# Second expert layer on the chosen pairs alone: rows scattered by expert through DRAM, in blocks of 128

## What is computed

```python
def _L1_ffn_ref(x, router_w, w1, w2, w3):     # 8 experts, hidden size 341
    logits = flat @ router_w.T
    probs = softmax(logits)
    topk_probs, topk_idx = top_k(probs, 2)
    topk_probs = topk_probs / (sum(topk_probs) + 1e-09)
    gates = einsum('nk,nke->ne', topk_probs, one_hot(topk_idx))
    h = silu(einsum('nc,ehc->neh', flat, w1)) * einsum('nc,ehc->neh', flat, w3)
    y = einsum('neh,ech->nec', h, w2)
    out = einsum('ne,nec->nc', gates, y)
```

## Time and profile before

| | before |
|---|---|
| median of 3 runs | 553.89 us (552.29 to 556.23) |
| span of the profiled execution | 552.8 us |
| PE busy | 487.0 us (88%), 1884 matrix instructions |
| DVE busy | 388.4 us (70%) |
| ACT busy | 268.6 us (49%) |
| POOL busy | 117.0 us (21%) |
| chain that ended last | PE 55%, DVE 24%, ACT 10%, issue 8% |

### The profile page before, as it was taken

How to read it: one execution, slowest core, us unless ns; L and a number is a source line. 1 busy time by engine, 2 the same in 40 slices (tenths; PEclk the granted TensorE clock), 3 DMA queues, 4 the chain that set the end, 5 groups by cost and what they waited for, 6 DMA issues and landing times.

```text
span 552.8 us, 6153 instructions
## 1 busy us (share of the span) xinstructions
PE 487.0 (88%) x1884; PEld 300.3 (54%) x1884; DVE 388.4 (70%) x709; ACT 268.6 (49%) x443; POOL 117.0 (21%) x171
## 2 busy tenths in 40 slices
PE   5496789868799989999799999899898998998996
PEld 3332545435356744556344444335466886776896
DVE  1997989766576832257648959767877967778674
ACT  5988787678675521032431222202225556565553
POOL 4000000000010000000000000885203554546564
PEclk9689589989799999989999999979998999999999
DMA  8880000000000010000000000332031221312340
GB/s 285 264 245 6 0 0 0 1 1 0 2 0 1 2 51 1 0 2 1 0 0 1 3 26 1 101 88 63 4 93 53 72 67 58 96 60 48 65 91 15
DMA packets 23640, 25.79 MB, mean 47 GB/s; under 512 B 2565, under 2 KB 18960, under 8 KB 23604
## 3 DMA queue, kind: packets, MB, share of 16 engines
q1 hardware_dynamic: 23604, 25.36, 16.1%
HBM read 24.61 MB, written 0.74 MB: 46 GB/s over the span
## 4 chain that ended last, share of the span: by engine, by line
PE 55%; DVE 24%; ACT 10%; issue 8%; DMA 1%; SPq 0%; POOLq 0%; DVEq 0%; POOL 0%; ACTq 0%
PE bank L1292 10%; PE bank L943 7%; PE bank L944 6%; PE bank L945 6%; PE bank L1122 4%; PE bank L1240 3%; DVE pr_ring L1887 3%; PE bank L1083 2%; PE bank L1281 2%; DVE y_units L1433 2%; DVE y_units L1444 2%; PE bank L1209 2%; PE bank L972 2%; DVE hr_ring L1703 2%; PE bank L1210 2%
## 5 line engine op out<-in xcount | busy, mean ns | idle before, releaser
L1292 PE MATMUL bank<-pr_ring,hW 128*128 128x512 f32 (+3 forms) x198 | 95.0, 565 | 6.6 <-DVE pr_ring L1887 6.0
L1887 DVE SCALAR_TENSOR_TENSOR pr_ring<-adjT,regR,bank 128x512 f32<-128x512 f32 (+3 forms) x99 | 64.7, 680 | 30.6 <-PE bank L1281 28.9
L1900 DVE TENSOR_TENSOR adjT<-bank,adjT 128x512 f32<-128x512 f32 (+1 forms) x66 | 41.3, 626 | 29.1 <-ACT bank L892 28.8
L1292 PEld LDWEIGHTS bank<-pr_ring,hW 128*128 128x128 f32 (+1 forms) x198 | 35.0, 194 | 36.6 <-DVE pr_ring L1887 18.8
L943 PE MATMUL bank<-z3hi,w13hi 128*128 128x512 f32 (+4 forms) x132 | 50.8, 385 | 3.6 <-DVE adjT L1900 3.6
L892 ACT ACTIVATE bank<-bank 128x512 f32<-128x512 f32 (+1 forms) x66 | 35.0, 531 | 36.3 <-PE bank L945 36.1
L944 PE MATMUL bank<-z3lo,w13hi 128*128 128x512 f32 (+4 forms) x132 | 48.9, 371 | 0.0
L945 PE MATMUL bank<-z3hi,w13lo 128*128 128x512 f32 (+4 forms) x132 | 48.8, 370 | 0.0
L604 POOL TENSOR_TENSOR prr_ring<-adjT,adjTr 128x512 fp32r<-128x512 f32 (+4 forms) x34 | 36.5, 1073 | 56.4 <-ACT adjTr L881 51.6
L972 PE MATMUL bank<-y_units,msg 128*128 128x512 f32 (+3 forms) x66 | 34.5, 655 | 15.7 <-DVE y_units L1454 15.7
L1083 PE MATMUL bank<-hr_ring,W2s 128*128 128x512 f32 (+1 forms) x96 | 45.5, 561 | 0.0
(11 more groups left out here) (270 smaller groups left out, 1025.3 us busy)
## 6 DMA issues: line engine op xcount, KB each, us to landing
adjT<-rows SPq DMA_DIRECT2D x16, 256.0 KB, 3.5
stage<-in_w SPq DMA_DIRECT2D x8, 341.0 KB, 2.9
adjT<-in_adjT SPq DMA_DIRECT2D x1, 2560.0 KB
adjT<-in_adjT SPq DMA_DIRECT2D x1, 1650.0 KB
adjT<-in_adjT SPq DMA_DIRECT2D x3, 512.0 KB, 6.9
adjT<-rows SPq DMA_DIRECT2D x8, 165.0 KB, 4.2
adjT<-in_adjT SPq DMA_DIRECT2D x1, 1024.0 KB
W1f<-in_W SPq DMA_DIRECT2D x1, 1024.0 KB, 11.7
```

Source lines behind the costliest of these rows:

```text
L1292: nc.tensor.matmul(B_ACC[:, 0:w], hW[0:r, j, k * P:(k + 1) * P], ring[0:r, 0:w], start=(k == 0 and j == 0), stop=(k == K - 1 and j == T - ...
L1887: nc.vector.scalar_tensor_tensor(out=pr_ring[0:r, 4 + p % R_RING, 0:w], in0=adjT[0:r, j, cols(c)], scalar=g_col[0:r, j, k:k + 1], in1=B_F[ ...
L1900: nc.vector.tensor_tensor(halves(sg, w), halves(B_H1[h_bank(q)][0:r, 0:w], w), gate_buf(n)[0:r, :, :], ALU.mult).then_inc(s["s_gated"], 1)
```

## The change

The second expert layer computes the chosen pairs of row and expert alone. Its steps after the change:

1. For each chunk, DVE marks the two experts of each row (`picks`), PE counts by products with a triangle of ones how many earlier rows chose each expert (`prefix`), and DVE makes of it two row numbers in a DRAM table for each row (`slots`). Chunks 0 and 1 are one group of 8 tiles with a table of its own (`xg0`), chunk 2 with 3 tiles is another (`xg1`). When the last chunk of a group is counted, DVE also makes the list of its blocks: where in the table each begins (`row_no`), and where its expert's weights begin (`wall_at`).
2. PE turns the rows back (`ztok`, `xtok`), and POOL scatters them into the table by indirect transfers, two per tile: 8 per full chunk, 6 for chunk 2.
3. A group has as many blocks of 128 rows as the worst routing needs: 23 and 13, 36 in all, run whatever the routing is. For each, SP reads the block's row number from memory and loads 128 rows (64 KB); PE transposes them, multiplies by w1 and w3 (f32, 341 columns each, at an address that PE reads from memory); ACT makes silu, DVE multiplies; PE transposes the three parts and multiplies by w2 (f32, three products of 128 columns); DVE copies the result out, SP stores it in a table `yg0` or `yg1`.
4. POOL gathers for each tile the two results of each row, 16 indirect transfers for the first group, 6 for the second, each group after its last block is stored; DVE adds them with their weights to `x` (`combine`), and SP stores the rows.

The four tables are filled with zeros near the beginning, 13.4 MB in all. The weights come straight from DRAM into `wall` and are not split. The layer norm and routing of all chunks stand ahead of the first block (`PRE_PE`, `PRE_ACT`, `PRE_DVE`), but for the last routing steps of chunk 2. Besides, some semaphores are shared and the transfer of `rw` counts on `gru_in`.

```diff
+HP = -(-H1 // 3)
+HT = [(k * HP, min(HP, H1 - k * HP)) for k in range(3)]
+WALL = 2 * H1 + len(HT) * P
+GROUPS = [(0, 8), (8, T)]
+GROUP_OF = [0, 0, 1]
+CAP = [b - a for a, b in GROUPS]
+BLOCKS = [(2 * (min(N, b * P) - a * P) + E * (P - 1)) // P for a, b in GROUPS]
+SPARE = [n - -(-2 * (min(N, b * P) - a * P) // P) for n, (a, b) in zip(BLOCKS, GROUPS)]
+TABLE = [E * n + m for n, m in zip(CAP, SPARE)]
+BLOCK = [(g, i) for g in range(2) for i in range(BLOCKS[g])]
+NB = len(BLOCK)
...
+HOLD = 4
...
+PRE_PE = [("gates", 1, 2), ("prefix", 1), ("mid", 1, 2), ("xtok", 0), ("xtok", 1), ("mean", 3, 2), ("var", 3, 2), ("logits", 5), ("ztok", 2)]
+PRE_ACT = [("support", 2), ("gates", 1, 2), ("new", 1, 2), ("xtok", 0), ("xtok", 1), ("center", 3, 2), ("table",), ("var", 3, 2), ("rank", 5),
+           ("ztok", 2), ("table", "silu")]
+PRE_DVE = [("ranks", 4), ("picks", 4), ("slots", 4), ("mid", 1, 2), ("blend", 1, 2), ("add", 1, 2), ("weights", 4), ("center", 3, 2),
+           ("scale", 3, 2), ("scores", 5)]
+PE1 = {3: [("prefix", 2)], 4: [("xtok", 2)]}
+ACT1 = {4: [("xtok", 2)]}
+DVE1 = {1: [("shares", 5)], 2: [("ranks", 5), ("picks", 5)], 4: [("slots", 5)], 5: [("weights", 5)]}
+DVE1.update({BLOCKS[0] + 4 + t: [("combine", t)] for t in range(GROUPS[0][1])})
...
+            sp.wait_ge(s["zpad_set"], 4)
+            for g in range(2):
+                n = TABLE[g]
+                k = next(i for i in range(1, n * P) if n * P % i == 0 and n * P // i <= T * P)
+                for table in (xg_d[g], yg_d[g]):
+                    sp.dma_start(table.rearrange("(p r) d -> p (r d)", p=P).rearrange("p (k n) -> p k n", k=k),
+                                 zeros[:, 0:n * P // k].unsqueeze(1).to_broadcast([P, k, n * P // k])).then_inc(s["tables_in"], 16)
...
+            def block_load(b):
+                g, i = BLOCK[b]
+                if i == 0:
+                    sp.wait_ge(s["list_set"], g + 1)
+                    sp.wait_ge(s[f"sent{g}"], 32 * (GROUPS[g][1] - GROUPS[g][0]))
+                at(sp, "xt_ps", b - XRING + 1)
+                row = sp.value_load(row_no[0:1, b:b + 1], min_val=0, max_val=(TABLE[g] - 1) * P)
+                sp.dma_start(xblk[:, b % XRING, :], xg_d[g][bass.ds(row, P), :]).then_inc(s[f"xb_in{b % XRING}"], 16)
+            def block_store(b):
+                g = BLOCK[b][0]
+                sp.wait_ge(s["y_set"], b + 1)
+                row = sp.value_load(row_no[0:1, b:b + 1], min_val=0, max_val=(TABLE[g] - 1) * P)
+                sp.dma_start(yg_d[g][bass.ds(row, P), :], yblk[:, b % YRING, :]).then_inc(s[f"y_out{b % YRING}"], 16)
+            for b in range(NB):
+                block_load(b)
+                if b >= HOLD:
+                    block_store(b - HOLD)
+            for b in range(NB - HOLD, NB):
+                block_store(b)
...
+            def send(c):
+                g = GROUP_OF[c]
+                pool.wait_ge(s["slot_set"], c + 1)
+                pool.wait_ge(s["htok_set"], C + c + 1)
+                for t in tiles(c):
+                    r = rows(t)
+                    for j in range(2):
+                        pool.indirect_dma_start(xg_d[g], bass.IndirectOffsetOnAxis(slot[0:r, t, j:j + 1], 0), ztok[0:r, t, :], None
+                                                ).then_inc(s[f"sent{g}"], 16)
+            def gather(g):
+                last = sum(BLOCKS[:g + 1])
+                for i in range(YRING):
+                    pool.wait_ge(s[f"y_out{i}"], 16 * len(range(i, last, YRING)))
+                for t in range(*GROUPS[g]):
+                    r = rows(t)
+                    for j in range(2):
+                        pool.indirect_dma_start(picked_y[0:r, t, j, :], None, yg_d[g], bass.IndirectOffsetOnAxis(slot[0:r, t, j:j + 1], 0)
+                                                ).then_inc(s[f"got{g}"], 16)
+            pool.wait_ge(s["tables_in"], 64)
+            for c in range(C):
+                send(c)
+            for g in range(2):
+                gather(g)
...
+            def block_turned(b):
+                at(pe, f"xb_in{b % XRING}", 16 * (b // XRING + 1))
+                at(pe, "xt_set", b)
+                nc.tensor.transpose(B_X[:, 0:P], xblk[:, b % XRING, :], ident[:, :]).then_inc(s["xt_ps"], 1)
...
+            def up(b, base):
+                at(pe, "xt_set", b + 1)
+                at(pe, "m_set", b - 1)
+                if b == 1:
+                    at(pe, "x3_ready", C)
+                x = xturned[:, b % 4, :]
+                nc.tensor.matmul(B_H1[b % 2][:, 0:H1], x, walls[:, bass.ds(base, H1)], start=True, stop=True).then_inc(s["h1_ps"], 1)
+                nc.tensor.matmul(B_H3[b % 2][:, 0:H1], x, walls[:, bass.ds(base + H1, H1)], start=True, stop=True).then_inc(s["h3_ps"], 1)
+            def hidden_turned(b):
+                at(pe, "m_set", b + 1)
+                at(pe, "ht_set", b)
+                for k in range(3):
+                    mm = nc.tensor.transpose(B_HT[0:HP, k * P:(k + 1) * P], hbuf[:, b % 2, k * HP:(k + 1) * HP], ident[:, :])
+                mm.then_inc(s["ht_ps"], 1)
+            def down(b, base):
+                at(pe, "ht_set", b + 1)
+                at(pe, "y_set", b)
+                for k, (_, r) in enumerate(HT):
+                    mm = nc.tensor.matmul(B_Y[:, 0:P], hturned[0:r, b % 2, k * P:(k + 1) * P],
+                                          walls[0:r, bass.ds(base + 2 * H1 + k * P, P)], start=(k == 0), stop=(k == 2))
+                mm.then_inc(s["y_ps"], 1)
...
+                pe.wait_ge(s["wall_in"], 80)
+                pe.wait_ge(s["list_set"], 1)
+                bases = {}
+                for b in range(2):
+                    block_turned(b)
+                for b in range(NB):
+                    if BLOCK[b] == (1, 0):
+                        pe.wait_ge(s["list_set"], 2)
+                    bases[b] = pe.value_load(wall_at[0:1, b:b + 1], min_val=0, max_val=(E - 1) * WALL)
+                    up(b, bases[b])
+                    if b + 2 < NB:
+                        block_turned(b + 2)
+                    if b:
+                        hidden_turned(b - 1)
+                    if b > 1:
+                        down(b - 2, bases.pop(b - 2))
+                    for task in PE1.get(b, []):
                         gat_side(task)
+                hidden_turned(NB - 1)
+                for b in (NB - 2, NB - 1):
+                    down(b, bases.pop(b))
...
+            def combine(t):
+                r, g = rows(t), int(t >= GROUPS[1][0])
+                if t == GROUPS[g][0]:
+                    at(dve, f"got{g}", 32 * (GROUPS[g][1] - GROUPS[g][0]))
+                    at(dve, "xtok_set", C if g else 2)
+                link(nc.vector.scalar_tensor_tensor(out=answer[0:r, t, :], in0=picked_y[0:r, t, 0, :], scalar=wab[0:r, t, 0:1],
+                                                    in1=x3tok[0:r, t, :], op0=ALU.mult, op1=ALU.add))
+                nc.vector.scalar_tensor_tensor(out=answer[0:r, t, :], in0=picked_y[0:r, t, 1, :], scalar=wab[0:r, t, 1:2],
+                                               in1=answer[0:r, t, :], op0=ALU.mult, op1=ALU.add).then_inc(s["answered"], 1)
+            def block_turned(b):
+                at(dve, "xt_ps", b + 1)
+                at(dve, "h3_ps", b - 3)
+                nc.vector.tensor_copy(xturned[:, b % 4, :], B_X[:, 0:P]).then_inc(s["xt_set"], 1)
+            def block_out(b):
+                at(dve, "y_ps", b + 1)
+                at(dve, f"y_out{b % YRING}", 16 * (b // YRING))
+                nc.vector.tensor_copy(yblk[:, b % YRING, :], B_Y[:, 0:P]).then_inc(s["y_set"], 1)
...
+                for b in range(NB):
+                    at(dve, "s_silu", b + 1)
+                    at(dve, "h3_ps", b + 1)
+                    nc.vector.tensor_tensor(hbuf[:, b % 2, 0:H1], hbuf[:, b % 2, 0:H1], B_H3[b % 2][:, 0:H1], ALU.mult).then_inc(s["m_set"], 1)
+                    if b + 2 < NB:
+                        block_turned(b + 2)
+                    if b > 1:
+                        block_out(b - 2)
+                    for task in DVE1.get(b, []):
                         gat_side(task)
```

More of the change, by code:

```diff
@@ L154 @@
-ACT1 = {0: [("gates", 1, 2)], 1: [("new", 1, 2)], 14: [("center", 3, 2)], 17: [("table",), ("var", 3, 2)],
-        30: [("table",), ("rank", C + 2)]}
-DVE1 = {0: [("mid", 1, 2)], 1: [("blend", 1, 2)], 2: [("add", 1, 2)], 5: [("ranks", C + 1)], 7: [("weights", C + 1)],
-        9: [("turn", C + 1)], 13: [("center", 3, 2)], 18: [("scale", 3, 2)], 29: [("scores", C + 2)], 31: [("shares", C + 2)],
-        32: [("ranks", C + 2)], 34: [("weights", C + 2)], 37: [("turn", C + 2)]}
-GBUF = 5
-SPLIT_AFTER = 4 * T + 5
@@ new lines, in prefix @@
+            def prefix(c):
+                at(pe, "tables_const", 7)
+                at(pe, "picked", c + 1)
+                take_side("pos_read", c + 1)
+                own, first = list(tiles(c)), GROUPS[GROUP_OF[c]][0]
+                n = len(own)
+                for i, t in enumerate(own):
```

(14 more changed lines are left out.)

474 lines of the change are left out of this document (207 added, 267 removed).

## The result

| | before | after |
|---|---|---|
| median | 553.83 us (552.29 to 556.23, 4 runs) | 672.41 us (668.82 to 677.91, 4 runs) |
| ratio | | 1.2145, 95% interval [1.2066, 1.2225] |
| span of the profiled execution | 552.8 us | 674.0 us |
| PE busy | 487.0 us (88%) | 512.6 us (76%) |
| DVE, ACT, POOL busy | 388.4, 268.6, 117.0 us | 349.6, 236.0, 55.7 us |

The account below looks back on a forecast made before the run. PE bound the old kernel; the new block loop would be bound by a store-to-load round trip. Loop start 439 + 11.4 + 33 x 6.2 + 2.5 + stall 6 + tail 17.2 gave 681, median 682 us, range 600 to 722.

Parts of the forecast that it names:

- The round trip: Block loop: y out, SP's reads and issues, load landing and PE's part in sequence, 6.2 us per iteration; chance 0.57.
- The landing: Block loop: a block's 64 KB load lands 2.4 us from its issue.
- PE's leg: Block loop, after the load: one transpose, three transposes and six products, 1.1 us, plus 0.2 to leave the array.
- C: Rival, block loop: PE's clock falls to the lower level, 7.3 us per iteration, total 714; chance 0.14.
- The number of trips: Block loop: three iterations at 3.8 us with loads ahead, then 33 at 6.2 us, 204.6 us.
- PE's pure work: Block loop: up products, transposes and down products take PE 2.3 us per block, 83 us for 36 blocks.
- Rival E: Not slower: loop at PE's pure work, 2.1 us per block, total 553; chance 0.05 including the missed cases around it.
- Prologue: Between attention and block 0: last chunk's GRU, layer norm and routing stand alone, so the loop starts at 439 us.
- D: Rival: POOL binds at 3.3 us per indirect DMA, lengthening first load, stall and tail, total 742; chance 0.07.
- The stall in the middle: At combine(0), end of iteration 27: DVE waits 6 us for group 0's gathers, and PE and SP with it.
- Tail: After the last block's copy: store, six gathers, landing, six DVE operations and output, 17.2 us.
- Attention stage: Splits leave DVE and POOL, PE gets 8 transposes and 14 small products: +1 us, bounds -2 and +3.

Follow-up runs that it names:

- the fillers: Three f32 products that nobody reads were put on PE in each of blocks 7 to 33 of the changed kernel; 646.1 us, ratio 1.166.
- the kernel with the second read: The changed kernel with SP reading the row number twice before each store, the first value dropped; 687.62 us, ratio 1.2405.

## Why the prediction came out right

**Bound and mechanism: right.** PE is not the bound of the loop any more, each `xblk` transpose waits for its load, SP's store waits for `yblk` and its load follows at once. `HOLD` shows it as cleanly as can be: 6.05, 3.00 and 2.3 us per block at 4, 5 and 6.

**The round trip: 6.2 predicted, 6.1 measured, by errors that cancel.** Of its terms, y out (0.30) and the store's issue (0.36 for 0.47) held. A register read is 0.27 + 0.15 us and 0.72 from its start to the following issue, for the 0.77 taken from the earlier trace rows. The Trainium skill ("DMA: Bandwidth & Descriptors", Latency and other measured facts) gives about 600 ns as the least for such a read; here the load itself is under that (0.27), and a second read right behind the first costs 0.55. The landing was mis-sized: 1.81 for 2.4, because I took the row of 192 KB for one of 64. The fit in the same page of the Trainium skill (Anatomy of one DMA), made for transfers that POOL issues, gives 2.15 for 64 KB; it was nearer and still high for these, which SP issues. PE's leg was mis-sized the other way: 2.4 us where 1.3 stood, since I priced it at full clock and put the low clock in a rival of its own. At full clock (from y out at 448.1 to y out at 453.6 of after) a trip is 5.5 us. C's share is the 26 us that the fillers gave back: with PE's clock near full the same round trip gives 646.

**The number of trips: 33 predicted, 30 measured.** The last block has no load to wait for, the first three take 2.05 and not 3.8, one at block 5 is short, and PE's register read costs nothing once the loop runs. Loop and last block take 214.2 us (441.0 to 655.3) for 224.5 booked.

**PE's pure work: 2.3 predicted, 2.26 measured** in the kernels that reach it. Rival E needed 2.1 by my sum. It was wrong to be so far away: with combine behind the loop and the transfers spaced, 2.26 gives 545 us. E's price had in it an 18.5 us wait that the order of the work decides, not the blocks.

**Prologue: near in sum, in a late profile.** The first transpose of a block starts at 439.3 (438 booked), the first up product at 441.0 (439). Three terms were off. The gates start at 413.8 and not 411.4, behind a copy of `ztok` and a load of ACT's table of 1.28 us; they run at half clock, 5 pairs at 1.10 us where the earlier trace rows have 0.55; and the 34 counts take 1 us and not 4.1, at 0.03 apiece:

```profile
411.38 0.59 ACT L803 COPY ztok<-bank 128x512 f32<-128x512 f32 x1 [2.71 <-PE bank L1293]
411.99 1.28 ACT L848 ACT_TABLE_LOAD   x1
413.28 0.43 ACT L839 COPY ge<-bank 128x330 f32<-128x330 f32 x1
```

**POOL's transfers: 1.2 us booked, 1.25 to 1.27 measured** start to start. D is out.

**The stall in the middle: right in size by luck.** The interval after block 27 is 12 us, 6 more than its neighbours, as booked. But DVE did not wait at combine(0), whose first operation follows the `yblk` copy at 610.34 with no idle time. SP had been slowed from 598.2 to 606.5, and the last gather began at 606.1, so when DVE came the rows were there. The wait that I described exists: 5.20 us in the kernel with the second read, for 6 booked. The step that failed is its price: I added it to the round trip in full, and there it lies beside SP's leg and the landing and costs next to nothing. It counts where the loop is faster (15.8 us at `HOLD = 5`). The 6 us in the sum were paid by the slow stretch of SP, which I had not foreseen.

**Tail: 17.2 booked, 18.75 measured** (655.25 to 674.0). The store goes out, six gathers start at 658.3, the last two take 1.36 us instead of 0.94, and DVE's six operations start at 668.8. **Attention stage: +1 booked, -3 measured.** It ends at 410.9, where it ended at 410.8, but in this profile it begins at 268.8 instead of 265.7. It lasts 142.1 us for 145.2, outside the bounds of -2 and +3, and in the other kernels it ends at 404.9 to 407.9. That the first block began within 2 us of the forecast is in part the lateness of this profile.

## What to carry to other kernels

When a loop moves data through DRAM between two engines, write down which load stands behind which store in the queue, and divide the whole round trip by the number of blocks that lie between them; here that one number was worth 100 us, and less work on PE was worth nothing until it was right. Price an engine that waits at the low clock, and a wait only by what it adds to the chain. And where a long row of indirect transfers stands beside a running pipeline and intervals are long without a reason, try it with waits between the transfers: in the fastest of these kernels that was worth 23 us, for a cause that is still open.

## What the runs showed of the hardware

- In four profiles, beside rows of 6 or 16 indirect transfers on POOL, each of up to 128 rows of 512 bytes and 1.25 us apart, the instruction streams of other engines are slow from some 5 us after the row's start: 0.7 us for SP instructions that take 0.02 to 0.3, and idle times of 3 to 6 us without a named releaser on ACT and PE. Spacing the same 22 transfers in the kernel with `HOLD = 6` took 23 us away. Other profiles with the same rows show nothing of it, so the row is not enough, and the recording of the profile is not excluded as the cause.
- Added work can raise the clock: 81 idle products brought the granted clock from 0.72 to 0.98 and made the kernel 26 us faster than the change.
- A 64 KB load lands 1.81 us after its issue in the trip shown (median 1.8), a store of 64 KB in 1.5.
- An indirect transfer of 128 rows of 512 bytes keeps POOL busy for 0.94 to 0.96 us, and the next starts 1.25 to 1.27 us after it; it lands 2.3 us (scatter) to 2.5 us (gather) after its issue in the kernel with the second read.
